# Selective scan, four experts and an FFN on one core: each token to its own expert, C by DMA, the product on GpSimd, the sum over states on TensorE

## The chip, the core and the metric

The kernel runs as one program on one core of a Trainium2 chip. The time is that of the device for one execution, in microseconds (us). A core has five engines that run their own instruction lists and meet only at semaphores: TensorE (PE; PEld is its weight load), VectorE (DVE), ScalarE (ACT), GpSimd (POOL) and SyncE (SP, which here only issues DMAs). Each list is executed in the order in which it is written: an instruction that waits holds back all behind it on that engine.

## The reference

Eight sequences x[b] of 1024 tokens, 128 channels. Layer one is a selective scan with 16 states per channel, followed by a mixture of four experts:

```
delta = softplus(x @ Wd + bd);  B = x @ WB + bB;  C = x @ WC + bC;  A = -exp(A_log)
h[s]  = clip(exp(min(delta*A[s], 2)) * h[s] + clip(delta*B[s], -2, 2) * x, -100, 100)   # over tokens
y     = sum_s h[s] * C[s] + x * D_param
route = softmax(y @ Wr + br);  top = argmax(route)
hid_e = silu(y @ up_w[e] + up_b[e]);  out_e = hid_e @ down_w[e] + down_b[e]      # 128 -> 512 -> 128
moe   = out_top * route[top]
x1    = norm(x + norm(y + moe) * ln_w + ln_b)
out   = norm(x1 + ffn(x1)),  ffn = (silu(x1 @ wg.T) * (x1 @ wu.T)) @ wdn.T        # int weights / 127, 384 hidden
```

The reference computes all four experts for each token and picks one. Only the picked one reaches the output.

## The kernel before

A sequence (batch) is one unit of work: tiles are 128 channels by 1024 tokens, or 128 tokens by 128 channels, eight of these to a batch. A batch goes through four stages, and an iteration runs four different ones side by side: `P` (projections, delta, B and C, and the bound that tells whether a clip could act) of batch i+1, `A` (the scan) of batch i, `B` (router, experts, first half of the norms) of batch i-1, `C` (norms and FFN) of batch i-2.

Stage A sets the frame. For each of the 16 states, PE spreads row s of B over all partitions (`psB`, two matmuls of 512 columns, line 382) and row s of C (`psC`, the same line); ACT makes `decay` (564); DVE multiplies `dx` into `psB` (662), runs the scan over tokens into `state` (849), and multiplies `state` by `psC` into `prod` (858); POOL adds `prod` to `yacc` (940), 15 times and a last time into `y`. `psB` and `psC` are single: the spread of state s+1 waits until the scan of s has read `psB`. On DVE the product of line 858 stands between the scan of s and the multiplication of s+1. `bc_parts` (822) and `dx` (823) are made at the batch's start.

Stage B computes all four experts for all tokens: for each of 2 halves of 512 tokens and 4 experts, `up` (437, four fp32 matmuls of 512 columns, each two instructions in the trace), `silu` (ACT 582, four of 128x512), `down` (444 for the bias, 451 for 16 fp32 matmuls of 128 columns), `weigh` (DVE 769, by 0 or the routing weight) and `mix` (POOL 893). The router's few columns ride in `y_turn` (430); lines 736 to 759 are its DVE part. The weights of all experts lie in SBUF from the start.

The order of each engine is a table per engine (`PE_STEPS`, `ACT_STEPS`, `DVE_STEPS`, `POOL_STEPS`) that hangs tasks on the 32 half steps of the scan. DMAs are few: per batch `xT` twice, `x` and the output.

The bound at the end of P (lines 716 to 732: `bound`, a scan as `majorant`, line 723, and a flag) chooses between the fast scan and a slow one token by token; in the profiled execution all scans are the fast ones.

## Time and profile before

| | |
|---|---|
| time, median of 3 runs | 1067.1 us (1066.87 to 1068.94) |
| time of the profiled execution | 1068.36 us |
| its span, first to last instruction | 1066.4 us |
| mean granted TensorE clock | 0.881 |
| busy share of the span, PE / DVE / ACT / POOL | 78% / 82% / 57% / 53% |
| DMA | 20.76 MB, 19 GB/s over the span |

An engine's share counts its own instructions, register and semaphore work left out. The span has a start (setup and stage P of batch 0), eight scans, and an end (what is left of batches 6 and 7), so shares over the whole span mix stretches with different limits; the table of stretches below is cut where the scans of the batches begin (the `dx` of line 823).

### The profile page before, as it was taken

To read this page: it belongs to the slowest core of one execution; us is meant where nothing else is said; L and a number is where in the kernel's file an instruction comes from. 1 tells how busy PE (TensorE), PEld (TensorE's weight loads), DVE (VectorE), ACT (ScalarE), POOL (GpSimd) and SP (SyncE) were. 2 spreads that over 40 slices of the span, in tenths; PEclk is the share of its full clock that TensorE was granted. 3 is DMA by queue.
4 is the path that set the end of the run, shared out by engine and by line. 5 is a ranking of instruction groups with operands and counts; after the bars stand their busy time and mean duration, and the time that the engine had idled before them with its cause. 6 is when DMAs were issued, how large, how long until landed. Compare 5 with 4: busy or idle time off the path is not lost.

```text
span 1066.4 us, 11980 instructions
## 1 busy us (share of the span) xinstructions
PE 835.7 (78%) x4059; PEld 521.1 (49%) x4120; DVE 878.6 (82%) x1173; ACT 609.3 (57%) x838; POOL 561.6 (53%) x412
## 2 busy tenths in 40 slices
PE   2354599768888789869897799869897789989973
PEld 1010256446555455546464455546554555657552
DVE  4999988699899998899899898999889999962332
ACT  5362177446866378456776278456775367525432
POOL 1255356555666465564576366564566466644232
PEclk8565699879998899979999899989998899989996
DMA  4100100010000100000000100001000100000000
GB/s 135 40 1 1 59 1 1 1 49 12 10 1 11 50 13 8 1 27 34 21 2 10 50 11 11 1 17 43 21 1 10 31 11 11 21 1 20 1 11 20
DMA packets 23046, 20.76 MB, mean 19 GB/s; under 512 B 2227, under 2 KB 19891, under 8 KB 22966
## 3 DMA queue, kind: packets, MB, share of 16 engines
q1 hardware_dynamic: 22966, 19.84, 5.9%
q8 instruction: 32, 0.52, 0.2%
q14 instruction: 48, 0.39, 0.1%
HBM read 15.64 MB, written 4.19 MB: 19 GB/s over the span
## 4 chain that ended last, share of the span: by engine, by line
DVE 37%; PE 34%; issue 13%; ACT 12%; POOL 2%; DVEq 1%; SPq 0%; DMA 0%; ACTq 0%; POOLq 0%
PE psU L437 15%; DVE state L849 11%; DVE psB L662 8%; PE psD L451 4%; ACT decay L564 3%; DVE prod L858 3%; PE psU L470 3%; PE psB L382 2%; DVE bst L791 2%; PE psU L471 2%; DVE weighed L769 2%; DVE inp L723 2%; PE psT L451 2%; PE psU L397 2%; PE psC L382 1%
## 5 line engine op out<-in xcount | busy, mean ns | idle before, releaser
L940 POOL TENSOR_TENSOR yacc<-prod,yacc 128x1024 f32<-128x1024 f32 x112 | 271.1, 2421 | 170.3 <-DVE prod L858 170.0
L849 DVE TENSOR_TENSOR_SCAN state<-decay,psB 128x1024 f32<-128x1024 f32 x128 | 292.7, 2287 | 13.2
L582 ACT ACTIVATE hid<-psU,upb_sb 128x512 f32<-128x512 f32 x256 | 175.7, 688 | 221.6 <-PE psU L437 221.4
L437 PE MATMUL psU<-y,up_sb 128*128 128x512 f32 x512 | 263.6, 652 | 1.8 <-ACT hid L582 1.8
L382 PE MATMUL psB<-bc_parts,sel 128*128 128x512 bf16 x233 | 83.3, 436 | 125.8 <-DVE state L849 100.6
L662 DVE TENSOR_TENSOR psB<-dx,psB 128x1024 f32<-128x1024 f32 x128 | 156.6, 1223 | 20.4 <-PE psB L382 19.3
L858 DVE TENSOR_TENSOR prod<-state,psC 128x1024 f32<-128x1024 f32 x128 | 155.9, 1218 | 20.8 <-PE psC L382 15.8
L451 PEld LDWEIGHTS psD<-down_sb,hid 128*128 128x128 f32 x1280 | 159.7, 203 | 7.1 <-issue 2.7
L437 PEld LDWEIGHTS psU<-y,up_sb 128*128 128x128 f32 x512 | 95.0, 205 | 139.4 <-ACT hid L582 93.3
L451 PE MATMUL psD<-down_sb,hid 128*128 128x128 f32 x1280 | 159.2, 286 | 0.2
L564 ACT ACTIVATE decay<-next_delta,a_sb 128x1024 f32<-128x1024 f32 x128 | 136.3, 1135 | 1.5 <-DVE state L849 1.4
L382 PEld LDWEIGHTS psB<-bc_parts,sel 128*128 128x128 bf16 x256 | 20.5, 100 | 165.3 <-DVE state L849 123.3
L893 POOL TENSOR_TENSOR moe<-moe,weighed 128x512 f32<-128x512 f32 x48 | 72.5, 1511 | 44.7 <-DVE weighed L769 42.4
L382 PE MATMUL psC<-bc_parts,sel 128*128 128x512 bf16 x222 | 78.0, 423 | 20.0 <-DVE prod L858 17.6
L451 PEld LDWEIGHTS psT<-down_sb,hid 128*128 128x128 f32 x768 | 89.5, 192 | 4.9 <-issue 2.7
L451 PE MATMUL psT<-down_sb,hid 128*128 128x128 f32 x768 | 89.6, 275 | 0.1
L900 POOL TENSOR_TENSOR minus_mean<-mv,minus_one 128x4 f32<-128x4 f32 x48 | 9.7, 202 | 105.8 <-DVE ve L799 105.8
L940 POOL TENSOR_TENSOR yacc<-prod,xD 128x1024 f32<-128x1024 f32 x8 | 18.8, 2354 | 74.8 <-DVE prod L858 62.7
L811 DVE SCALAR_TENSOR_TENSOR hh<-psU,hh 128x512 f32<-128x512 f32 x48 | 32.6, 690 | 28.7 <-PE psU L471 22.2
L382 PEld LDWEIGHTS psC<-bc_parts,sel 128*128 128x128 bf16 x256 | 23.4, 103 | 61.3 <-DVE prod L858 35.4
L588 ACT ACTIVATE x1h<-psT 128x512 fp32r<-128x512 f32 x16 | 9.6, 597 | 74.5 <-PE psT L460 74.4
L602 ACT ACTIVATE hh<-psU 128x512 f32<-128x512 f32 x48 | 28.5, 597 | 38.8 <-PE psU L471 38.6
(118 smaller groups left out, 1134.6 us busy)
## 6 DMA issues: line engine op xcount, KB each, us to landing
xT_sb<-in_xT SPq DMA_DIRECT2D x8, 512.0 KB, 3.3
x_again<-in_xT SPq DMA_DIRECT2D x8, 512.0 KB, 4.3
xt<-in_x SPq DMA_DIRECT2D x16, 256.0 KB, 3.4
out<-x SPq DMA_DIRECT2D x16, 256.0 KB, 2.3
up_sb<-in_up_w SPq DMA_DIRECT2D x1, 1024.0 KB, 7.7
hid<-in_wg SPq DMA_DIRECT2D x1, 192.0 KB, 2.5
hid<-in_wu SPq DMA_DIRECT2D x1, 192.0 KB, 3.3
hid<-in_wdn SPq DMA_DIRECT2D x1, 192.0 KB, 3.5
```

Source lines behind the costliest of these rows:

```text
L382: mm = pe.matmul(half(ps, c), sel[:, which * S + s, :], half(bc_parts, c), start=True, stop=True)
L437: pe.matmul(bank[banks[f]][:, :], up_sb[:, e, f * 128:(f + 1) * 128], half(y, c), start=True, stop=True).then_inc(filled[banks[f]], 1)
L451: mm = pe.matmul(bank[d][:, j * 128:(j + 1) * 128], hid[:, k % 2, f, j * 128:(j + 1) * 128], down_sb[:, e * NF + f, :], start=False, stop= ...
L470: pe.matmul(bank[u][:, :], w[:, m * 128:(m + 1) * 128], x1h[:, :], start=True, stop=False)
L564: nc.scalar.activation(decay[:, s % NDECAY, :], next_delta[:, :], ACT.Exp, scale=a_sb[:, s:s + 1]).then_inc(decay_ready, 1)
L582: nc.scalar.activation(hid[:, k % 2, f, :], bank[u][:, :], ACT.Silu, bias=upb_sb[:, (k % E) * NF + f:(k % E) * NF + f + 1]).then_inc(drain ...
L662: v.tensor_tensor(psB[:, :], dx[:, :], psB[:, :], ALU.mult).then_inc(inp_ready, 1)
L811: v.scalar_tensor_tensor(out=hh[:, m, :], in0=bank[up][:, :], scalar=INV127, in1=hh[:, m, :], op0=ALU.mult, op1=ALU.mult).then_inc(drained ...
L849: v.tensor_tensor_scan(state[:, :], decay[:, s % NDECAY, :], psB[:, :], 0.0, ALU.mult, ALU.add).then_inc(state_ready, 1)
L858: v.tensor_tensor(prod[:, s % NPROD, :], state[:, :], psC[:, :], ALU.mult).then_inc(prod_ready, 1)
L893: g.tensor_tensor(dst, ytok[:, c * NJ:(c + 1) * NJ, 0:D] if e == 0 else dst, weighed[:, k % 2, :, :], ALU.add).then_inc(mixed, 1)
L940: g.tensor_tensor((y if s == S - 1 else yacc)[:, :], prod[:, s % NPROD, :], (xD if s == 0 else yacc)[:, :], ALU.add).then_inc(added, 1)
```

## The change

- **Experts.** Each token goes to its own expert only. Router: `yT_turn`, `logits`, then `rank` (PE, with a triangular matrix of ones: each token's place within its expert) and `slots` (DVE, eight small instructions). Tokens are sorted into blocks of 128 that belong to one expert; 1024 tokens make at most 8 + 3 = 11 blocks, and 11 are always computed. POOL writes the rows to DRAM by 8 indirect DMAs of 128 rows (`scatter`), SP reads them back as blocks (`rows`, 3 DMAs), PE turns them (`sort_turn`), `up` / `silu` / `down` / `result` run per block of 128 tokens, SP stores the results (`store`, 3 DMAs), POOL fetches each token's row by 8 indirect DMAs (`gather`), DVE combines (`combine`: output times weight plus y, 8 instructions). Weights aren't resident: SP reads a block's expert number into a register and loads 128x1156 fp32 (592 KB, up, down and biases) into one of three buffers, 11 per batch.
- **C and the product.** Rows of C go to DRAM once per batch (ACT's DMA) and SP reads each back to all 128 partitions (`c_wide`, 512 KB, 16 per batch, 3 buffers). POOL multiplies `state` by `c_wide` into `prod` (3 state buffers, 3 product buffers).
- **The sum over states.** PE adds the products by transposing them into one accumulator in PSUM (`psY`, 8 transposes of 128x128 per state, one more set for x*D_param), which also turns them to tokens; ACT copies it (`y_copy`).
- **Smaller parts.** `bc_parts`, `x_again`, the `majorant` scan and `weigh` / `mix` go. The bound on h becomes (delta + 1/min|A|)*|x|*max|B| (`widen`, one more pass of `bound`); the flag goes by a DMA of 2 KB. The rest of x1 in the FFN is formed on PE (`x_rest`) and copied by ACT, and the FFN's residual is added on PE (16 more matmuls of 128 columns per batch). The output's DMAs go from ACT.
- **The order.** One table per engine, SP included, now lists tasks with the batch they belong to; there are no half steps any more, and a task of the next batch may stand anywhere.

The core of the diff (of the tables that set the order, only the scan's part on DVE is shown):

```diff
-NDECAY = 8
-NPROD = 4
+NDECAY, NSTATE, NPROD, NC, NW = 6, 3, 3, 3, 3
...
+    (-2, "ff_mul", 0, 0), (0, "scan", 11), (-2, "ff_mul", 0, 1), (-2, "ff_mul", 0, 2), (-2, "stats", 1, 1), (1, "dx"),
+    (1, "over"), (0, "scan", 14), (1, "flag"), (0, "scan", 15), (1, "scan", 0), (-2, "ff_mul", 1, 0),
+    (-2, "ff_mul", 1, 1), (-2, "ff_mul", 1, 2), (1, "scan", 1), (-2, "stats", 1, 2), (1, "scan", 2), (1, "scan", 3),
+    (1, "scan", 4), (1, "scan", 5), (0, "router_shift"), (1, "scan", 6), (0, "slots"), (-1, "combine", 0),
+    (-1, "stats", 0, 0), (1, "scan", 7), (0, "router_pick"), (-1, "combine", 1), (1, "scan", 8), (-1, "stats", 1, 0),
...
+            def load_c(c, s):
+                g = S * c.n + s
+                if s == 0:
+                    sp_.wait_ge(c_stored, 16 * (c.n + 1))
+                wait(sp_, prod_ready, g - NC + 1)
+                sp_.dma_start(c_wide[:, g % NC, 0:c.w], c_rows[c.n % 2, s:s + 1, 0:c.w].to_broadcast([D, c.w])
+                              ).then_inc(c_in[g % NC], 16)
...
+                if name == "weights":
+                    (k,) = args
+                    q = c.blocks0 + k
+                    if k == 0:
+                        sp_.wait_ge(blocks_ready, c.n + 1)
+                    wait(sp_, result_ready, q - NW + 1)
+                    e = sp_.value_load(block_expert[0:1, c.n % 2, k:k + 1], min_val=0, max_val=E - 1)
+                    sp_.dma_start(weights[:, q % NW, :], w_pack[bass.ds(e, 1), :, :].rearrange("o p w -> p (o w)")
+                                  ).then_inc(weights_in[q % NW], 16)
...
+            def add_turned(c, term, src, first, last, done):
+
+                for j in range(c.tiles):
+                    mm = pe.matmul(psY[:, j, :], src[:, j * ROWS:(j + 1) * ROWS], ident[:, :], is_transpose=True,
+                                   start=(first and j % NJ == 0), stop=last, skip_group_check=True)
+                mm.then_inc(done, 1)
+
+            def add_state(c, s):
+
+                g = S * c.n + s
+                pe.wait_ge(prod_ready, g + 1)
+                add_turned(c, s, prod[:, g % NPROD, :], False, s == S - 1, summed)
...
-                if name == "up":
-                    c, e = divmod(args[0], E)
-                    for f in range(NF):
-                        fill(it, banks[f], stage, task, f // 2)
-                        pe.matmul(bank[banks[f]][:, :], up_sb[:, e, f * 128:(f + 1) * 128], half(y, c),
-                                  start=True, stop=True).then_inc(filled[banks[f]], 1)
+                if name == "up":
+                    (k,) = args
+                    (u,) = banks
+                    q = c.blocks0 + k
+                    pe.wait_ge(weights_in[q % NW], 16 * (q // NW + 1))
+                    pe.wait_ge(turned, c.groups0 + k // 4 + 1)
+                    fill(u, c, task)
+                    for f in range(NF):
+                        mm = pe.matmul(bank[u][:, f * ROWS:(f + 1) * ROWS], weights[:, q % NW, f * 128:(f + 1) * 128],
+                                       yT_sorted[:, k * ROWS:(k + 1) * ROWS], start=True, stop=True)
+                    mm.then_inc(filled[u], 1)
...
+                    pe.matmul(bank[d][:, 0:D], ones_row[:, :], weights[0:1, q % NW, W_DOWNB:W_DOWNB + D],
+                              start=True, stop=False)
+                    for f in range(NF):
+                        mm = pe.matmul(bank[d][:, 0:D], hid[:, k % 2, f, :],
+                                       weights[:, q % NW, W_DOWN + f * D:W_DOWN + (f + 1) * D],
+                                       start=False, stop=(f == NF - 1))
+                    mm.then_inc(filled[d], 1)
...
+                if name == "silu":
+                    (k,) = args
+                    q = c.blocks0 + k
+                    u = f"U{k % 2}"
+                    act.wait_ge(filled[u], fills(u, c, ("up", k)))
+                    for f in range(NF):
+                        ins = nc.scalar.activation(hid[:, k % 2, f, :], bank[u][:, f * ROWS:(f + 1) * ROWS], ACT.Silu,
+                                                   bias=weights[:, q % NW, W_UPB + f:W_UPB + f + 1])
+                    ins.then_inc(drained[u], 1)
+                if name == "result":
+                    (k,) = args
+                    (d,) = banks_of(c, ("down", k))
+                    act.wait_ge(filled[d], fills(d, c, ("down", k)))
+                    wait(act, stored, 16 * c.groups0)
+                    nc.scalar.activation(result[:, k, :], bank[d][:, 0:D], ACT.Copy).then_inc(drained[d], 1)
+                    act.wait_ge(drained[d], fills(d, c, ("down", k)))
+                    act.sem_inc(result_ready, 1)
...
+                if name == "combine":
+                    (h,) = args
+                    dve.wait_ge(gathered, 16 * (c.tiles0 + c.tiles))
+                    dve.wait_ge(router_steps, 7 * (n + 1))
+                    wait(dve, affine_steps[h], 3 * c.with_half[h])
+                    for j in range(c.hj):
+                        jj = h * NJ + j
+                        ins = v.scalar_tensor_tensor(out=moe[:, jj, :], in0=chosen_out[:, jj, :],
+                                                     scalar=top_w[:, n % 2, jj:jj + 1], in1=ytok[:, n % 2, jj, :],
+                                                     op0=ALU.mult, op1=ALU.add)
+                    ins.then_inc(mixed[h], 1)
...
+                if name == "prod":
+                    (s,) = args
+                    g = S * n + s
+                    if g == 0:
+                        pool.wait_ge(setup_dve, SETUP)
+                    pool.wait_ge(state_ready, g + 1)
+                    pool.wait_ge(c_in[g % NC], 16 * (g // NC + 1))
+                    wait(pool, summed, g - NPROD + 1)
+                    g_.tensor_tensor(prod[:, g % NPROD, w], state[:, g % NSTATE, w], c_wide[:, g % NC, w], ALU.mult
+                                     ).then_inc(prod_ready, 1)
...
+                if name == "scatter":
+                    (j,) = args
+                    if j == 0:
+                        pool.wait_ge(zeroed, 32)
+                        pool.wait_ge(slots_ready, n + 1)
+                        pool.wait_ge(y_copied, n + 1)
+                        for m in range(3):
+                            wait(pool, sorted_in[m], 16 * c.with_group[m])
+                        wait(pool, scattered, 16 * c.tiles0)
+                    g_.indirect_dma_start(rows_in, bass.IndirectOffsetOnAxis(slot[:, n % 2, j:j + 1].bitcast(U32), 0),
+                                          ytok[:, n % 2, j, :], None).then_inc(scattered, 16)
+                if name == "gather":
+                    (j,) = args
+                    if j == 0:
+                        pool.wait_ge(stored, 16 * (c.groups0 + len(c.groups)))
+                        for h in range(2):
+                            wait(pool, mixed[h], c.with_half[h])
+                    g_.indirect_dma_start(chosen_out[:, j, :], None, rows_out,
+                                          bass.IndirectOffsetOnAxis(slot[:, n % 2, j:j + 1].bitcast(U32), 0)
+                                          ).then_inc(gathered, 16)
```

In the rows below a name is followed by what is written and what is read; x4 means four such in a row.

ScalarE, in a batch in the middle, where the experts' silu stands between the decays (before: `hid` is silu, `decay` is exp, `x1h` a copy, `hh` the FFN's silu, `moe` a norm):

```order
L588 ACTIVATE x1h<-psT 128x512
L582 ACT_TABLE_LOAD
L582 ACTIVATE hid<-psU,upb_sb 128x512 x8
L602 ACTIVATE hh<-psU 128x512 x3
L594 ACTIVATE moe<-moe,shift,rstd 128x128 x4
L564 ACT_TABLE_LOAD
L564 ACTIVATE decay<-next_delta,a_sb 128x1024 x4
L582 ACT_TABLE_LOAD
L582 ACTIVATE hid<-psU,upb_sb 128x512 x8
```

And now (`result` is the copy of a block's output):

```order
L710 ACT_TABLE_LOAD
L710 ACTIVATE decay<-delta,a_sb 128x1024
L739 ACTIVATE yT_sorted<-psD 128x512
L749 ACT_TABLE_LOAD
L749 ACTIVATE hid<-psU,weights 128x128 x8
L757 ACTIVATE result<-psT 128x128
L739 ACTIVATE yT_sorted<-psD 128x384
L710 ACT_TABLE_LOAD
L710 ACTIVATE decay<-delta,a_sb 128x1024
L757 ACTIVATE result<-psT 128x128
L749 ACT_TABLE_LOAD
L749 ACTIVATE hid<-psU,weights 128x128 x4
```

The decays, four or five in a row before, now come one at a time between the silus, and a table load stands at each turn: 9 in an iteration before, 16 now.

GpSimd, before, around the end of a scan (`moe<-moe,weighed` is `mix`):

```order
L881 TENSOR_TENSOR bnd<-bnd,zb 128x512 x2
L940 TENSOR_TENSOR yacc<-prod,yacc 128x1024
L893 TENSOR_TENSOR moe<-moe,weighed 128x512
L940 TENSOR_TENSOR yacc<-prod,yacc 128x1024
L893 TENSOR_TENSOR moe<-moe,weighed 128x512
L940 TENSOR_TENSOR y<-prod,yacc 128x1024
```

And now, where the gathers and the first scatters stand among the products:

```order
L1070 TENSOR_TENSOR prod<-state,c_wide 128x1024
L1099 DMA chosen_out<-rows_out,slot 128x128 x3
L1070 TENSOR_TENSOR prod<-state,c_wide 128x1024
L1099 DMA chosen_out<-rows_out,slot 128x128 x5
L1070 TENSOR_TENSOR prod<-state,c_wide 128x1024
L1091 DMA rows_in<-ytok,slot 1408x128
L1076 TENSOR_TENSOR bnd<-bcf,parts 128x1024
```

The 16 additions of a batch have become 16 products, the additions of the experts' outputs are gone, and 16 indirect DMAs are issued from this engine; the first gather waits for the last store of its batch, with the products behind it.

TensorE, before, in the same part of a batch (`psB`, `psC` the spreads, 437 `up`, 451 `down`):

```order
L382 MATMUL psC<-bc_parts,sel 128x512 x2
L437 MATMUL psU<-y,up_sb 128x512 x4
L444 MATMUL psT<-bias_down,sel 128x512
L451 MATMUL psT<-down_sb,hid 128x128 x16
L382 MATMUL psB<-bc_parts,sel 128x512 x2
L382 MATMUL psC<-bc_parts,sel 128x512 x2
```

And now (480 adds a product, 473 is the spread of B, 596 and 599 `down`, 586 `up`):

```order
L473 MATMUL psB<-parts,sel 128x512 x2
L480 MATMUL psY<-ident,prod 128x128 x8
L596 MATMUL psT<-weights,ones_row 128x128
L599 MATMUL psT<-weights,hid 128x128 x4
L586 MATMUL psU<-yT_sorted,weights 128x128 x4
L608 MATMUL psD<-ident,attn 128x128 x4
L586 MATMUL psU<-yT_sorted,weights 128x128 x4
L473 MATMUL psB<-parts,sel 128x512 x2
```

Each piece of expert work between two spreads has become smaller, the spread of C is gone, and the addition of a product has come in; a spread has one order place only, so an addition that waits for POOL ahead of it holds it back.

## Rows read from the trace of the kernel before

**Rows 1.** The page's part 4: the chain that ended last, by engine.
```profile
DVE 37%; PE 34%; issue 13%; ACT 12%; POOL 2%; DVEq 1%; SPq 0%; DMA 0%; ACTq 0%; POOLq 0%
```

**Rows 2.** Stretches: start:end and length, busy us of each engine (instructions), clock, DMA.
```profile
core 0: us, PE busy (x) PEld busy (x) DVE busy (x) ACT busy (x) POOL busy (x), PEclk, DMA share, GB/s
0.00:31.70 31.70, 7.74 (x27) 3.51 (x27) 16.39 (x36) 20.07 (x22) 4.82 (x7) 0.78 0.39 113
31.70:119.00 87.30, 36.98 (x89) 8.43 (x91) 83.25 (x64) 29.77 (x30) 40.94 (x19) 0.54 0.04 13
119.00:233.80 114.80, 92.43 (x432) 57.20 (x439) 98.32 (x101) 67.87 (x83) 63.90 (x37) 0.87 0.04 14
...
476.10:596.30 120.20, 99.48 (x507) 63.43 (x515) 108.63 (x146) 76.53 (x105) 70.73 (x51) 0.94 0.06 18
...
838.40:953.00 114.60, 102.54 (x510) 66.30 (x519) 101.94 (x135) 61.10 (x92) 63.20 (x48) 0.93 0.04 13
953.00:1066.40 113.40, 87.08 (x467) 59.12 (x469) 33.32 (x123) 47.66 (x87) 35.01 (x47) 0.91 0.04 12
```

**Rows 3.** Groups of lines, 476.1 to 596.3: busy us, mean ns | idle before, releaser.
```profile
L849 DVE TENSOR_TENSOR_SCAN state<-decay,psB 128x1024 f32<-128x1024 f32 x16 | 36.6, 2287 | 1.7
L940 POOL TENSOR_TENSOR yacc<-prod,yacc 128x1024 f32<-128x1024 f32 x14 | 34.0, 2431 | 16.8 <-DVE prod L858 16.8
L437 PE MATMUL psU<-y,up_sb 128*128 128x512 f32 x64 | 32.0, 634 | 0.6 <-ACT hid L582 0.6
L582 ACT ACTIVATE hid<-psU,upb_sb 128x512 f32<-128x512 f32 x32 | 21.9, 688 | 27.7 <-PE psU L437 27.7
L662 DVE TENSOR_TENSOR psB<-dx,psB 128x1024 f32<-128x1024 f32 x16 | 19.6, 1224 | 2.9 <-PE psB L382 2.7
L858 DVE TENSOR_TENSOR prod<-state,psC 128x1024 f32<-128x1024 f32 x16 | 19.5, 1218 | 2.8 <-PE psC L382 2.5
L451 PE MATMUL psD<-down_sb,hid 128*128 128x128 f32 x160 | 18.7, 275 | 0.0
...
L893 POOL TENSOR_TENSOR moe<-moe,weighed 128x512 f32<-128x512 f32 x6 | 9.6, 1592 | 3.7 <-DVE weighed L769 3.4
...
L382 PE MATMUL psC<-bc_parts,sel 128*128 128x512 bf16 x27 | 8.7, 389 | 1.8 <-DVE prod L858 1.4 <-issue 0.2
...
L769 DVE TENSOR_TENSOR weighed<-psD,top_w 128x512 f32<-128x512 f32 x5 | 3.4, 673 | 0.0
...
L916 POOL TENSOR_TENSOR moe<-moe,lnb_sb 128x512 f32<-128x512 f32 x2 | 2.6, 1278 | 0.2
...
L723 DVE TENSOR_TENSOR_SCAN inp<-sp,bnd 128x1024 f32<-128x1024 f32 x1 | 2.3, 2282 | 0.0
...
L905 POOL TENSOR_TENSOR shift<-minus_mean,rstd 128x4 f32<-128x4 f32 x6 | 1.2, 200 | 1.0 <-POOL rstd L902 1.0
```

**Rows 4.** Timeline of ScalarE: start, duration us, what.
```profile
546.46 1.64 ACT L594 ACTIVATE moe<-moe,shift,rstd 128x128 f32<-128x128 f32 x4
548.11 1.28 ACT L564 ACT_TABLE_LOAD   x1
549.41 4.27 ACT L564 ACTIVATE decay<-next_delta,a_sb 128x1024 f32<-128x1024 f32 x4
```

**Rows 5.** Timeline of TensorE: a spread of B at either clock, four transposes.
```profile
66.30 0.60 PE L382 MATMUL psB<-bc_parts,sel 128*128 128x512 bf16 x2 [1.56 <-DVE state L849]
...
87.24 1.04 PE L382 MATMUL psB<-bc_parts,sel 128*128 128x512 bf16 x2 [2.49 <-DVE state L849]
...
1024.48 0.60 PE L460 MATMUL psT<-ident_wr,x 128*128 128x128 f32 x4
```

**Rows 6.** Line 756 alone (VectorE, two SBUF inputs): duration ns, min/median/max.
```profile
L756 DVE TENSOR_TENSOR top_w<-rcode,rsmall x8: 141/2147/2152, 140.3 to 965.0; 128x32 f32<-128x32 f32 x8
```

**Rows 7.** DMA: the queue's total (MB, share of 16 engines), and issues with us to landing.
```profile
q1 hardware_dynamic: 22966, 19.84, 5.9%
...
xT_sb<-in_xT SPq DMA_DIRECT2D x8, 512.0 KB, 3.3
```

1273 lines of the change are left out of this document (713 added, 560 removed), and 32 rows, old and new, of tables (ACT_STEPS, DVE_STEPS, PE_STEPS, POOL_STEPS).

## The prediction, made before the changed kernel was run

> **What bounds the kernel now.** I read three views. The chain [rows 1] names DVE (37%) and PE (34%) and leaves POOL at 2%: POOL's long waits for products cost nothing. The table of stretches [rows 2] gives the limit by stage. A full batch takes 120.2 us, of which DVE works 108.6, PE 99.5, ACT 76.5, POOL 70.7, so DVE is the bound and is idle 11.6 us. Batch 0's scan takes 87.3 us, also DVE (83.3), at a low clock (0.54) with PE only 37.0 us busy. The second takes 114.8, the last 114.6, the start 31.7, the end 113.4; the five between average 120.9 (from 233.8 to 838.4). The groups of lines [rows 3] say what each engine does in a full batch. DMA is at 6%, no limit.
>
> **DVE.** Gone: 16 products, 19.5 us; 8 `weigh` at 0.67, 5.4; the majorant scan, 2.3 [rows 3]. Smaller ones gone (the reduction after that scan, the copy of parts, the subtraction and residual of the FFN, two router instructions) I put at 8 us, from DVE's 1218 ns for 1024 columns and 673 for 512 [rows 3] and line 756's 2.1 [rows 6]. New: two more half passes of `bound` (1.4 by the 673), 8 `slots` instructions and the flag's, small ones of 0.14 to 0.2 (2.0 in all, by line 756's shortest), 8 `combine` of 128 columns, between that 0.14 and the 0.67 (2.3). 108.6 - 35.2 + 5.7 = 79.
>
> One cost stands only indirectly in the trace. Line 756 has two SBUF operands and 32 columns; it took 0.14 us once and 2.15 at the median [rows 6], which is close to a whole POOL addition (2.4) [rows 3]. Twelve new DVE instructions have two SBUF operands (8 `combine`, 1 in the router, 3 in `slots`), and POOL will be busy three quarters of the time. From nothing to 12 x 2.0 = 24 us; most will meet POOL in the middle of something or not at all, and I take 6. DVE: 85.
>
> The Trainium skill says it as a rule ("SBUF — State Buffer", Who interferes with whom): a VectorE instruction with two SBUF inputs contends with a GpSimd one that reads SBUF, and one of the two is blocked for the other's whole length. The trace agrees (2.15 against 0.14 us). By the rule scan and multiplication, each with an operand in PSUM, stay free.
>
> **The gap between scans.** `psB` is single. Before, the product (1.2 us) covered the spread of the next row of B: 0.60 us at the high clock, 1.04 at the low [rows 5], and DVE waited only 2.9 us a batch for it [rows 3]. Now DVE goes from scan to multiplication with nothing between at four places of its table (15 to 0, 2 to 3, 3 to 4, 4 to 5): 0.7 each with the semaphore, 3 us. At the others another task covers. A spread held behind work of PE is in the idle time, which I keep at 12 of the 11.6. DVE's own sum is then 85 + 3 + 12 = 100.
>
> **PE.** Gone per batch: `up` 32.0; `down`, of which 160 instructions take 18.7, so all 256 take 29.9; the spreads of C 8.7; the biases 3 (8 of about 0.38, the length of a spread's half) [rows 3]; the old turn of y, 16 instructions at 0.12 or more, 2. That is 76 of 99.5. New: adding is 17 x 8 transposes. Four took 0.60 us [rows 5], so one more costs about 0.11 (`down` gives 18.7/160 = 0.117) and eight about 1.04: 17.7 us. A block's `up` is 4 fp32 matmuls, 8 instructions: 0.27 for the first and 7 x 0.117, 1.1; its `down` 10, 1.3; 11 blocks, 26.6. Turns, ranks, logits, the FFN's extra parts: some 70 instructions at 0.117, 8 us. 99.5 - 76 + 52 = 76 us at clock 0.94.
>
> **ACT.** Gone: 32 silu, 21.9 [rows 3]; the three copies of the old turn at about 0.5, 1.4. New: 44 silu of 128 columns. A 128-column norm in a group of four takes 1.64/4 = 0.41 [rows 4], a 512-column silu 0.688; 384 columns fewer at about 0.83 ns leave 0.37, less in a row; I take 0.31: 13.6. Eleven `result` 3.1, copies to turned tiles, y and x1 (9 of about 0.6) 5.3. Table loads: 16 for 9, 7 x 1.28 = 9.0. 76.5 - 23.3 + 31.0 = 84 us. ACT is the closest second.
>
> A load's cost is 1.28 here: it starts 0.01 us after the norm before it ends and the decay 0.02 after it [rows 4]. The Trainium skill ("ScalarE: Activation LUTs", What ACT_TABLE_LOAD costs) has 1283 ns and about 1380 ns of drain, 2.66 in all. By that, ACT would have 16 x 1.38 = 22 us more. The trace shows no such gap.
>
> **POOL.** Additions become products of the same size, 39 us for 39. `mix` goes: 8 calls, 9.6 and 2.5 us, 12. 70.7 - 12 = 58.6. New: 16 indirect DMAs to issue. No row has one; the nearest are POOL's smallest instruction, 0.20 us, and its largest, 2.43 [rows 3]. I take 1.28, that of a 128x512 instruction, for descriptors of 128 rows: 20 us, so 79 (62 to 98). The first gather waits for the last store of its batch; behind it wait the products from state 4 on, for them PE's additions, and, three states on, the scan. The Trainium skill ("DMA: Bandwidth & Descriptors", Specifications) gives about 1 us to the first byte on GpSimd's path; by that as an issue price POOL would be 75.
>
> **SP and DMA.** 27 big loads (16 of 512 KB, 11 of 592 KB), with rows, stores, x and out: 19 MB per batch. Before, 19.84 MB took 5.9% of 1066 us on all 16 engines [rows 7]: 315 GB/s, so 60 us per batch, 58% used. Loads of 512 KB land in 3.3 us alone [rows 7], and each C row has two states, over 10 us. Hidden, if the same 4 KB row read 128 times is no slower; if each load went alone, 16 x 3.3 + 11 x 4 = 97 us, still under the period.
>
> **The sum.** A full batch: DVE's 100, with three other engines at 76 to 84 that in-order lists couple to it; before, PE at 83% already stood in that idle time. I add 3: **103 us**, for 120.9. Batch 0's scan: 87.3 - 19.5 - 5 (copy, majorant) + 16 bare gaps of 1.1 at the low clock = 80. Second and last stretch in proportion (0.855): 98 each. The start stays 31.7: setup and the same projections. The end: 113.4 holds 62 us of dense `up` and `down`, now 11 blocks at about 2.4 us through PE, ACT, PE, ACT, 27: -35. It gains four DMA trips of about 3.3 (scatter, rows, store, gather), 13; 16 issues on POOL, 20, of which 2 overlap; router and slots in a chain, 3. About 112. Sum: 31.7 + 80 + 98 + 5 x 103 + 98 + 112 = 934.7; with the 2.0 us that lie outside the span (1068.36 - 1066.4), 936.7, and the profiled run was 1.3 above the median. **Forecast 935 us**, 12% faster.
>
> **Rivals.**
> 1. Waits overlap better. Port conflicts near nothing, POOL at 65: 92 us a batch. 31.7 + 75 + 88 + 460 + 88 + 100 + 2 = 845. For it: DVE has only 79 us of work. Against: four engines at 75 to 85 leave little slack. Chance 0.20.
> 2. POOL becomes the bound. At 2.4 us per indirect DMA it works 97 us; with 12 idle, 110 a batch: 31.7 + 80 + 103 + 550 + 103 + 120 + 2 = 990. For it: nothing here prices these DMAs, and the products wait behind them. Not faster than before only from (120 - 12 - 58.6)/16 = 3.1 us each. Chance 0.15.
> 3. The slower side: the clock stays down. In the scan of batch 0 PE was 42% busy and had 0.54, the lower level of 1.2 GHz most of the time; at 77 to 83% busy it had 0.87 to 0.94 [rows 2]. Work on PE falls by a quarter and consists of small pieces between waits. At the low level a spread takes 1.04 for 0.60 [rows 5], 1.7 times; PE's 76 become 129, with 12 idle 141 a batch: 31.7 + 85 + 125 + 705 + 135 + 125 + 2 = 1209. It decides from a mean clock of about 0.66, where PE's 76 become 108. Against: 76 of 103 is 74% busy, nearer to the stretches with 0.87. Chance 0.10, with 0.02 for POOL beyond 3.1 us: slower 0.12.
> 4. ACT becomes the bound, because a turn from exp to silu and back costs twice the load's row where it comes 16 times (ACT must finish one thing before the next, and no longer does four decays in between): 16 x 1.3 more, 84 + 21 + 11 = 116 a batch; 31.7 + 80 + 110 + 580 + 110 + 118 + 2 = 1032. Against: no such gap in the rows of the load [rows 4]. Chance 0.02. The Trainium skill's drain, above, is this rival.
> 5. It comes out even (a mix of 2 and 3): 0.02. That the change doesn't do what it says would show as scans by the slow path, hundreds of us each; its conditions are those of before. Under 0.01.
>
> The forecast has the remaining 0.49. Its own range is 96 to 110 us a batch, 880 to 990. For 8 in 10 I go from 848 (rival 1) to 1055, past rivals 2 and 4, leaving out most of rival 3. About 0.2% is what this measurement can tell from no change. Faster 0.86, same 0.02, slower 0.12.
>
> **What would show it.** Stretches between the `dx` of neighbouring batches of 96 to 110 us, DVE 82 to 90 busy in each, ACT 80 to 88, PE 70 to 85 at a clock of 0.8 or more, POOL 72 to 86. DVE instructions with two SBUF inputs far above 0.2 us would show the port's cost; DVE's waits before line 1040 for PE, the gap's; POOL's for C, a DMA limit; line 1099's issues, rival 2. I am wrong if the period follows PE at a clock under 0.7, if scans wait for products that stand behind gathers, or if C rows arrive late.

## The result, and the profile after

| | before | changed |
|---|---|---|
| time, median (4 runs each on the same chip) | 1068.0 us (1066.9 to 1069.5) | 1100.7 us (1099.3 to 1106.3) |
| ratio, 95% interval | | 1.031 (1.028 to 1.035), slower |
| span of the profiled execution | 1066.4 us | 1104.5 us |
| mean granted TensorE clock | 0.881 | 0.779 |

The forecast was 935 us, and the time lies outside its range (848 to 1055). The profiled execution of the changed kernel is the longest of its four (1106.3 us; the others 1099.3 to 1101.3). The tables of stretches say where the time is. Those of the changed kernel, cut at the first multiplication of each batch's scan (columns as in [rows 2]):

```profile
0.00:34.70 34.70, 9.18 (x27) 3.96 (x27) 12.35 (x36) 20.63 (x22) 4.82 (x6) 0.74 0.36 100
34.70:116.80 82.10, 41.40 (x182) 27.78 (x183) 64.19 (x49) 28.50 (x28) 44.26 (x18) 0.65 0.31 109
116.80:220.20 103.40, 66.09 (x373) 50.59 (x372) 74.94 (x68) 50.25 (x78) 51.43 (x27) 0.73 0.48 159
565.90:683.60 117.70, 87.12 (x541) 69.63 (x540) 88.92 (x132) 82.87 (x142) 75.50 (x59) 0.80 0.50 160
802.50:917.00 114.50, 80.85 (x512) 65.58 (x511) 76.42 (x116) 66.39 (x125) 67.90 (x56) 0.81 0.48 149
917.00:1104.50 187.50, 99.91 (x577) 78.63 (x575) 35.72 (x165) 62.07 (x161) 58.72 (x76) 0.74 0.24 73
```

and two of the kernel before, cut the same way (a full batch, and what follows the end of the last scan):

```profile
477.40:597.60 120.20, 99.51 (x508) 63.43 (x515) 108.60 (x144) 76.53 (x105) 70.73 (x51) 0.94 0.06 19
942.00:1066.40 124.40, 96.04 (x506) 65.06 (x509) 37.87 (x129) 51.34 (x94) 38.61 (x49) 0.90 0.04 11
```

Up to the end of the last scan the changed kernel is 25 us ahead (917.0 for 942.0). The drain behind it takes 187.5 us for 124.4, 63 more, and 63 - 25 = 38 is the difference of the spans. A full batch was to fall from 120 to 103 us and fell to 117.7: VectorE lost 19.7 us of work (108.6 to 88.9) and gained 17.2 of idle time (11.6 to 28.8). What the reader is to see is that in the full batch no engine is busy more than 76% of the time. The waits of that stretch (total us, times, longest) spread over all of them:

```profile
POOL prod L1070 <- DVE state L1043: 36.1, 8, 8.9
PEld psB L473 <- DVE state L1043: 16.3, 5, 6.6
DVE psB L1040 <- PE psB L473: 13.6, 7, 4.3
PE psB L473 <- DVE state L1043: 13.5, 5, 5.7
ACT moe L769 <- POOL shift L1113: 13.0, 2, 8.1
DVE holder L912 <- PE psT L532: 8.1, 1, 8.1
```

TensorE waits 13.5 us for a scan before it may spread the next row of B, and VectorE waits 13.6 for spreads, for 2.7 before [rows 3]: each in turn is late for the other. The groups of lines of that stretch that answer to [rows 3] (busy us, mean ns, idle before):

```profile
L1043 DVE TENSOR_TENSOR_SCAN state<-decay,psB 128x1024 f32<-128x1024 f32 x16 | 36.6, 2287 | 1.6
L1040 DVE TENSOR_TENSOR psB<-dx,psB 128x1024 f32<-128x1024 f32 x16 | 19.6, 1226 | 14.5 <-PE psB L473 13.6 <-issue 0.4 <-DVE clip_flag L922 0.2
L586 PE MATMUL psU<-yT_sorted,weights 128*128 128x128 f32 x88 | 13.2, 303 | 0.0
L599 PE MATMUL psT<-weights,hid 128*128 128x128 f32 x88 | 12.7, 288 | 0.0
L596 PE MATMUL psT<-weights,ones_row 1*128 1x128 f32 x22 | 5.3, 320 | 1.2 <-ACT hid L749 0.8 <-ACT result L757 0.4
L749 ACT ACTIVATE hid<-psU,weights 128x128 f32<-128x128 f32 x44 | 12.5, 368 | 3.7 <-PE psU L586 3.4
L1091 POOL DMA_INDIRECT rows_in<-ytok,slot x8 | 8.4, 1054 | 3.6 <-issue 3.6
L903 DVE TENSOR_TENSOR parts<-bnd,parts 32x1024 bf16<-32x1024 f32 x1 | 6.0, 5957 | 0.0
```

Most prices of the prediction hold in these rows: `up` and `down` with its bias (line 596) 31.2 us for 26.6, which at the measured clock (0.80 for 0.94) would be 31.3; silu 12.5 for 13.6; an indirect DMA about 1.25 us from one issue to the next (in its usual place 0.96 and 0.30 of idle time) for 1.28. One row was not priced at all: L903 (`bc_low`, two SBUF inputs) took 5.96 us for a work of 1.22. GpSimd held it, and for longer than one of its instructions. The timelines of VectorE and GpSimd there (start, duration):

```profile
638.81 5.96 DVE L903 TENSOR_TENSOR parts<-bnd,parts 32x1024 bf16<-32x1024 f32 x1
644.80 0.69 DVE L1023 SCALAR_TENSOR_TENSOR hh<-psU,hh 128x512 f32<-128x512 f32 x1
```

```profile
637.74 4.72 POOL L1070 TENSOR_TENSOR prod<-state,c_wide 128x1024 f32<-128x1024 f32 x2
642.43 1.25 POOL L1124 TENSOR_TENSOR moe<-moe,lnw_sb 128x512 f32<-128x512 f32 x1
643.76 2.13 POOL L1126 TENSOR_TENSOR moe<-moe,lnb_sb 128x512 f32<-128x512 f32 x1
```

Two products and L1124 stand back to back, and L903 gets through only at about 643.7, where L1126 has to wait for L1124's result. L1126 then takes 2.13 us, for 1.25 to 1.28 in the drain: it is now the held one.

The drain, in the chain of the changed kernel (start, duration; left out are pieces under 0.9 us and repeats): batch 6's last blocks, its gathers, its mixing and norm; batch 7's scatters with batch 6's affine steps between them; batch 7's blocks with the loads of their weights; its gathers; its norms.

```profile
935.56 1.10 PE psT L599 x8
...
940.72 0.95 POOL chosen_out L1099
...
948.21 5.24 DMA chosen_out<-rows_out,slot
...
961.10 1.05 POOL rows_in L1091
962.18 1.27 POOL moe L1124
...
976.28 2.23 DMA rows_in<-ytok,slot
978.53 2.80 DMA y_sorted<-rows_in
...
989.62 4.90 DMA weights<-in_w_pack
...
1000.25 5.83 DMA weights<-in_w_pack
...
1045.66 2.59 DMA chosen_out<-rows_out,slot
```

The same view of the kernel before has, in its drain, dense TensorE work back to back:

```profile
969.96 7.43 PE psU L437 x16
...
977.45 3.73 PE psD L451 x32
...
986.47 7.45 PE psU L437 x16
```

TensorE is busy about as long in both drains (99.9 and 96.0 us, at clocks of 0.74 and 0.90). Before, that was 77% of the drain; now it is 53%.

### The profile page after: what moved, and what is told of

Read it like the earlier page. It is cut to its first block, busy times and chain, and to the rows that moved or that the text cites. A ratio compares the mean times of both kernels' runs of the same rounds, so it can differ in the third digit from the quotient of the medians.

```text
span 1104.5 us, 13970 instructions
## 1 busy us (share of the span) xinstructions
PE 723.8 (66%) x4320; PEld 563.2 (51%) x4320; DVE 705.4 (64%) x1078; ACT 636.3 (58%) x1108; POOL 601.4 (54%) x468
## 4 chain that ended last, share of the span: by engine, by line
PE 39%; DVE 24%; issue 13%; ACT 7%; DMA 6%; POOL 6%; SPq 1%; DVEq 1%; ACTq 0%; POOLq 0%
DVE state L1043 11%; PE psY L480 7%; PE psU L586 7%; DVE psB L1040 6%; PE psT L599 6%; PE psB L473 5%; PE psD L640 4%; DMA weights<-in_w_pack 3%; PE psT L596 2%; PE psU L624 2%; DVE bst L1008 2%; PE psU L625 2%; POOL rows_in L1091 1%; DVE moe L991 1%; ACT decay L710 1%
## 5 line engine op out<-in xcount | busy, mean ns | idle before, releaser
L1070 POOL TENSOR_TENSOR prod<-state,c_wide 128x1024 f32<-128x1024 f32 x128 | 305.2, 2388 | 280.4 <-DVE state L1043 265.7
L1043 DVE TENSOR_TENSOR_SCAN state<-decay,psB 128x1024 f32<-128x1024 f32 x128 | 292.7, 2287 | 13.6 <-DVE psB L1040 0.5
L1040 DVE TENSOR_TENSOR psB<-dx,psB 128x1024 f32<-128x1024 f32 x128 | 157.0, 1227 | 134.3 <-PE psB L473 124.4
L473 PE MATMUL psB<-parts,sel 128*128 128x512 bf16 x256 | 100.1, 482 | 159.7 <-DVE state L1043 159.6
L480 PE MATMUL psY<-ident,prod 128*128 128x128 f32 x1024 | 169.8, 327 | 28.8 <-POOL prod L1070 28.8
L480 PEld LDWEIGHTS psY<-ident,prod 128*128 128x128 f32 x1024 | 153.8, 174 | 47.4 <-POOL prod L1070 30.7
L710 ACT ACTIVATE decay<-delta,a_sb 128x1024 f32<-128x1024 f32 x128 | 142.2, 1142 | 11.0 <-DVE state L1043 5.9
L749 ACT ACTIVATE hid<-psU,weights 128x128 f32<-128x128 f32 x352 | 99.8, 369 | 51.2 <-PE psU L586 49.8
L586 PE MATMUL psU<-yT_sorted,weights 128*128 128x128 f32 x704 | 105.5, 302 | 8.4 <-DMA weights<-in_w_pack 6.8
L586 PEld LDWEIGHTS psU<-yT_sorted,weights 128*128 128x128 f32 x704 | 98.7, 217 | 15.9 <-DMA weights<-in_w_pack 8.8
L599 PE MATMUL psT<-weights,hid 128*128 128x128 f32 x704 | 104.7, 293 | 0.0
L599 PEld LDWEIGHTS psT<-weights,hid 128*128 128x128 f32 x704 | 87.6, 196 | 10.9 <-issue 0.7
L1091 POOL DMA_INDIRECT rows_in<-ytok,slot x64 | 65.1, 1017 | 39.5 <-issue 39.5
```

What stands on the lines that cost most here:

```text
L473: mm = pe.matmul(tokens(psB, c, h), sel[:, s, :], parts[:, c.n % 2, h * HALF:h * HALF + c.hw], start=True, stop=True)
L480: mm = pe.matmul(psY[:, j, :], src[:, j * ROWS:(j + 1) * ROWS], ident[:, :], is_transpose=True, start=(first and j % NJ == 0), stop=last, ...
L586: mm = pe.matmul(bank[u][:, f * ROWS:(f + 1) * ROWS], weights[:, q % NW, f * 128:(f + 1) * 128], yT_sorted[:, k * ROWS:(k + 1) * ROWS], st ...
L599: mm = pe.matmul(bank[d][:, 0:D], hid[:, k % 2, f, :], weights[:, q % NW, W_DOWN + f * D:W_DOWN + (f + 1) * D], start=False, stop=(f == NF ...
L710: nc.scalar.activation(decay[:, g % NDECAY, w], delta[:, n % 2, w], ACT.Exp, scale=a_sb[:, s:s + 1]).then_inc(decay_ready, 1)
L749: ins = nc.scalar.activation(hid[:, k % 2, f, :], bank[u][:, f * ROWS:(f + 1) * ROWS], ACT.Silu, bias=weights[:, q % NW, W_UPB + f:W_UPB + ...
```

## Experiments

All are timed against the kernel before on the same chip; the changed kernel's ratio is 1.031. "Period" is the mean of the last five of the seven intervals between first multiplications, the first two being shorter in every kernel: 116.5 us in the changed kernel, 120.9 before. "Drain" is the time from the end of the last scan. Both are read from one profiled execution each, and two executions with the same steady part (e7 and e10) differ by 2.2 us in the period, so differences under about 2 us say little by themselves.

**e1: an order of its own for the end.** Behind the last sum of batch 7 each engine follows a written list.

```diff
 # GpSimd, behind batch 7's last product
-gather(6) 0..7, scatter(7) 0, rstd, scatter(7) 1, affine(6), rstd, rstd, scatter(7) 2..7, ...
+scatter(7) 0..7, rstd, gather(6) 0..7, rstd, affine(6), ...
 # TensorE
-up/down(6) .. 10, yT_turn(7), logits(7), rank(7), x_turn(6), ff_up(6), sort_turn(7), up/down(7), ...
+yT_turn(7), logits(7), rank(7) between blocks of 6, up/down(7) 0..10, ff_up(6), ff_down(6), ...
```

> Same work; only the order of what is left after the last state's sum of batch 7 is written out anew on every engine: batch 7's router and its eight scatters go ahead of batch 6's gathers, batch 7's experts run without a stop, batch 6's two feed-forward halves follow them, in the hole in which batch 7's gathers and norms run. The steady part (to the end of the last scan, 917.0 us of the changed kernel's span) is untouched. Theory A (the whole loss against the kernel before, 187.5 us of drain for 124.4, is the order of the end: a steady order's places kept where no scan is left): the drain falls from 187.5 to 145-160 us, total 1060-1075. Rival B (the end is long because its chain of gathers, norms and matmuls at a low clock is long whatever the order): drain 180 or more, total within 1% of 1100.7.

Measured: ratio 1.034 (1.031 to 1.038), drain 183.9. Expectation A failed and rival B's numbers came, but this order had a fault of its own. GpSimd did its scatters at 941 to 951, but ScalarE's list then had batch 6's first norm ahead of results that batch 7's blocks wait for, and that norm waited for batch 6's gathers, now 14 us later.

**e2: one transpose of eight.**

```diff
-for j in range(c.tiles):
+for j in range(c.tiles if term < 0 or term == S - 1 else 1):
     mm = pe.matmul(psY[:, j, :], src[...], ident[:, :], is_transpose=True, ...
```

> Of every state but the last, one of the eight transposes is issued (the other seven columns of the sum are left out), so TensorE has 105 short matmuls less in a batch, 12 us at 0.11 each and up to 26 at the 0.25 of the low clock, out of 87 us busy of 117.7. All waits, DMAs and other engines' work stay. Theory A (TensorE's list in order, with the sums in front of the next B spread, sets the pace of a batch): period from 117.7 to 103-109 us, total 1010-1040. Rival B (VectorE blocked by GpSimd, or ScalarE, sets the pace): period 115-118, total 1085-1101. Rival C (fewer columns bring the granted clock down further and give the time back): clock below 0.75 in a batch and total within 1% of 1100.7.

Measured: ratio 1.019 (1.016 to 1.022), period 115.5, drain 181.0. The full batch:

```profile
560.50:676.80 116.30, 74.33 (x430) 55.37 (x435) 90.27 (x133) 82.74 (x142) 75.56 (x59) 0.77 0.52 163
```

TensorE has 12.8 us less work in it, the batch takes 1.4 us less, and the whole kernel 12.4 (1088.3 for 1100.7), half of it in the drain. TensorE's own work does not set the pace; theory A, as I had put it, is wrong. The numbers are those of rival B.

**e3: no silu.**

```diff
-nc.scalar.activation(hid[...], bank[u][...], ACT.Silu, bias=...)
+nc.scalar.activation(hid[...], bank[u][...], ACT.Identity, bias=...)
-nc.scalar.activation(hh[...], bank[u][...], ACT.Silu, scale=INV127)
+nc.scalar.activation(hh[...], bank[u][...], ACT.Copy, scale=INV127)
```

> Silu of the experts and of the gates is left out (Identity and Copy in its place, same shapes), so that no activation table has to be changed for it: some 10 to 12 loads of 1.28 us less in a batch, ScalarE from 83 to 68-72 us of 117.7. Theory A (TensorE's list and the single B tile couple the engines, ScalarE is only passed through by the experts' chain): period 113-117, total 1070-1095. Rival B (the table loads stand in the chain that sets the pace: state decays late, experts' silu late): period 103-109, total 1000-1040. If there are as many loads as before: no change.

Measured: ratio 1.027 (1.024 to 1.030), period 115.4, drain 184.8. Table loads fell from 106 to 17, and ScalarE by 17.6 us in the full batch (65.3 of 116.3); the batch by 1.4, the whole kernel by 4.4 (1096.3). ScalarE does not set the pace either.

**e4: two indirect DMAs for sixteen.**

```diff
 if name == "scatter": ...
+    if j > 0:
+        return
     g_.indirect_dma_start(rows_in, ...)          # the same for the gathers
```

> Of the eight scatters and eight gathers of a batch one each is issued (tokens of the other seven tiles are not moved, the mixing reads tile 0's rows), so GpSimd has 14 indirect DMAs less in a batch, 14 x 1.26 = 17.6 us of 75.5 busy of 117.7, and blocks VectorE's two-input instructions less. Theory A (TensorE's list sets the pace): period 112-117 us and drain shorter by 15-25 us (gathers and scatters stand alone there), total 1040-1085. Rival B (GpSimd's products arrive late behind series of indirect DMAs, or its use of the port blocks VectorE: 5.6 us for one 1.2 us instruction): period 100-108, total 960-1010.

Measured: ratio 0.983 (0.978 to 0.987), period 111.9, drain 167.7. GpSimd has 12.6 us less in the full batch, which is 6.2 shorter. It is between the two expectations: nearer to A in the period, and the drain is 19.7 shorter, as A had it. L903 is no longer held (its line: ns, min/median/max):

```profile
L903 DVE TENSOR_TENSOR parts<-bnd,parts x8: 1222/1277/1517, 21.6 to 735.1; 32x1024 bf16<-32x1024 f32 x8
```

for, in the changed kernel,

```profile
L903 DVE TENSOR_TENSOR parts<-bnd,parts x8: 1221/5606/8545, 21.7 to 757.9; 32x1024 bf16<-32x1024 f32 x8
```

so up to 4.3 of the 6.2 us may be that, and the cut does not separate it from the queue of GpSimd. (The profiled execution is the longest of four, 1058.0 us for a median of 1049.9.)

**e5: the B tile is free one scan earlier.**

```diff
-wait(pe, state_ready, S * c.n + s)                 # before a spread
+wait(pe, inp_ready, S * c.n + s)
-v.tensor_tensor(psB[:, w], dx[:, n % 2, w], psB[:, w], ALU.mult)
+v.tensor_tensor(inp[:, w], dx[:, n % 2, w], psB[:, w], ALU.mult)
-v.tensor_tensor_scan(state[...], decay[...], psB[:, w], ...)
+v.tensor_tensor_scan(state[...], decay[...], inp[:, w], ...)
```

> VectorE's multiplication writes a tile in SBUF instead of the B tile in PSUM in place, and the next B spread waits for that multiplication and no more for the scan behind it: the single B tile is free one scan (2.3 us) earlier for each state. Orders and everything else as in the changed kernel. Theory A (the single B tile and the spreads queued behind TensorE's bunches set the pace; 20 us a batch in which TensorE waits for a scan before a spread, 14 in which VectorE waits for a spread): period from 117.7 to 100-108 us, total 980-1030. Rival B (the spread's place in TensorE's list behind other work that waits for something else, not the tile, is what holds): period 113-118, total 1065-1100. Rival C (the scan now reads two inputs from SBUF and is blocked by GpSimd as L903 was): scans above 2.3 us, total above 1105.

Measured: ratio 1.087 (1.083 to 1.092), period 128.1: rival C. The profiled execution took 1176.8 us, the other three 1155.3 to 1164.4, so the period is some 2 us on the long side. Two lines of that execution, of all 128 scans and 48 shifts:

```profile
L1045 DVE TENSOR_TENSOR_SCAN state<-decay,inp 128x1024 f32<-128x1024 f32 x128 | 342.0, 2672 | 13.6 <-DVE inp L1042 0.5
...
L1115 POOL TENSOR_TENSOR shift<-minus_mean,rstd 128x4 f32<-128x4 f32 x48 | 35.5, 739 | 8.2 <-POOL rstd L1112 7.7 <-PE psY L481 0.3 <-DMA c_wide<-c_rows 0.2
```

The scan takes 0.39 us more than with its input in PSUM (2287 ns above), and GpSimd pays more than VectorE: its work in the full batch goes from 75.5 to 92.3 us. So the second SBUF input costs both engines, and what the single tile costs stays open, since this edit changes both.

**e6: the same tasks in other places.** Only the five tables differ. The new places are chosen with this trace's durations as costs (1.25 us for an indirect DMA, 1.3 for a table load, VectorE held while GpSimd works, 4 to 5 for a transfer). Part of GpSimd's table:

```diff
-gather 0, gather 1, gather 2, prod 4, gather 3 .. gather 7, prod 5, scatter 0, bc_rest, rstd, prod 6,
-scatter 1, affine 0, prod 7, rstd, rstd, scatter 2 .. scatter 7, prod 8, prod 9, affine 1, prod 10, ...
+gather 0 .. gather 6, prod 4, gather 7, scatter 0, prod 5, scatter 1, prod 6, rstd, scatter 2,
+affine 0, scatter 3, rstd, scatter 4 .. scatter 7, rstd, prod 7, bc_rest, prod 8, affine 1, prod 9, ...
```

> The same instructions, all five order lists rewritten (each list keeps each batch's own sequence of states, blocks and halves; what changes is where one batch's work stands between the other's). The new places are chosen by the changed kernel's own durations: 1.25 us for an indirect DMA, 1.3 us for an activation table load, VectorE's two-input instructions held while GpSimd works, TensorE at a clock of 0.8, 4 to 5 us for a transfer. Theory A (the loss is in the lists' places, fixed for other durations than these, so that engines of 75-89 us busy wait for each other for 29 us of 117.7): same busy times, period 101-108 us, drain 170-190, total 985-1040. Rival B (the period is set by a resource the lists don't show, such as the clock, which falls as TensorE's work gets denser, or DMA latency under load): period 114 or more, total 1070-1110.

Measured: ratio 0.973 (0.970 to 0.976), that is 1038.0 us; period 108.8, drain 184.3. A full batch:

```profile
528.60:638.60 110.00, 81.97 (x541) 65.97 (x542) 84.14 (x133) 75.66 (x135) 76.58 (x58) 0.86 0.54 175
```

Moving tasks alone took 7.7 us off the period: theory A holds for the steady part, though the period is 0.8 us above its range. But busy times were not the same. Table loads fell from 106 to 70, VectorE was held less (84.1 for 88.9), and TensorE's clock rose (0.86 for 0.80), against what rival B supposed. Seen from VectorE, over the five intervals of the period, 4.2 of the 7.7 us are work (88.3 to 84.1) and 3.4 are idle time (28.1 to 24.7). So over half of the gain goes with instructions that are held less, and not with engines that wait less for each other; the places decide both, and this run does not separate them.

**e7: places once more, and a half waits for its own gathers.**

```diff
-gathered = sem("gathered")
+gathered = [sem(f"gathered{h}") for h in range(2)]
-dve.wait_ge(gathered, 16 * (c.tiles0 + c.tiles))
+dve.wait_ge(gathered[h], 8 * (c.tiles0 + c.tiles))
```

> The order lists of e6 gone over once more with what its trace added (GpSimd's elementwise work is itself held while VectorE has two inputs from SBUF: 1.71 us for 1.26 in L1125 of e6; about 0.1 us more for each wait that has to be woken), and the mixing of each half waits for its own four gathers, not for all eight. Theory A (places in the lists set the pace): busy times as in e6 (PE 80, VectorE 84, ScalarE 76, GpSimd 76), period from 108.9 to 100-105 us, drain 175-185, total 985-1025. Rival B (e6 has taken what order can give; the rest is waking times and the clock): period 107-110, total 1030-1045.

Measured: 1018.0 us (1017.1 to 1021.4), ratio 0.953 (0.951 to 0.954); period 107.6 in the profiled execution, its last two intervals 105.7 and 105.2; drain 174.7. The first of these two:

```profile
532.50:638.20 105.70, 79.65 (x547) 64.71 (x545) 85.74 (x133) 75.27 (x136) 76.52 (x59) 0.89 0.57 181
```

VectorE is idle 20.0 us, for 28.8; over the five intervals 21.9, for 28.1, and its work is 85.7. By the total this is theory A; by the period of its own profile it is rival B, by that of e10, 105.4 with the same steady part, nearly A. Tables and semaphore changed together, so the gain over e6 is not divided between them. This version is faster than both kernels: 4.7% below before, 7.5% below the changed kernel (1018.0/1100.7).

**e8: e7 with an end of its own.** From state 8 of batch 7 on, a written list again, without e1's mistake.

```diff
 # GpSimd, behind batch 7's last product, in e8
+rstd, scatter(7) 0..4, gather(6) 0, scatter(7) 5..7, gather(6) 1..7, rstd, affine(6), ...
```

> As e7, and what is left from state 8 of batch 7 on is put in an order of its own: batch 7's first scatters ahead of batch 6's gathers, its experts in one run, batch 6's feed-forward halves behind them, and no norm of batch 6 on ScalarE ahead of a result that batch 7's experts wait for, which is what stopped e1 (its second expert block waited until 6's gathers had landed). Theory A (in the end the lists' places cost as much as in the steady part): drain of 150-165 us, total 12 to 25 below e7. Rival B (the end is one chain through the router, scatters, sorted rows, eleven blocks, gathers, norms and two feed-forward halves of the last batch, which no order shortens): within 8 us of e7.

Measured: ratio 0.962 (0.960 to 0.964), 1027.6 us, 9.6 slower than e7. The drain is 168.9, 5.8 shorter, but the last scan ends 10.6 us later; the list has blocks of batch 6 ahead of spreads and sums of batch 7, which is the likely reason and was not tested. Neither expectation; the drain alone speaks for rival B.

**e9: L903 with one input.**

```diff
-v.tensor_tensor(parts[96:128, n % 2, w], rest[96:128, w], parts[96:128, n % 2, w], ALU.subtract)
+v.tensor_scalar(parts[96:128, n % 2, w], rest[96:128, w], 1.0, None, ALU.mult)
```

> The changed kernel with the third bf16 part of B and C made from one input (the subtraction of the second part is left out, the result is the rounded remainder itself), so that VectorE's L903 has one SBUF input and is not held by GpSimd: 1.2 us for 5.6. Theory A (a place in the lists sets the pace, and VectorE waits 9 to 13 us a batch around there anyway): period 115-118, total within 0.7% of 1100.7. Rival B (blocked VectorE instructions are on the path of every batch): 4.4 us less a batch, total 1060-1075. If L903 still takes over 3 us, it is not the second input that holds it.

Measured: ratio 1.028 (1.025 to 1.030), period 115.0, theory A's numbers. But it did not do what it was meant to:

```profile
L903 DVE TENSOR_SCALAR parts<-bnd x8: 690/4901/5426, 22.0 to 751.1; 32x1024 bf16<-32x1024 f32 x8
```

With one SBUF input the instruction is faster when free (0.69 for 1.22 us) and still held when GpSimd works. So the run tests neither theory, and how much of the period the hold costs is not settled by it.

**e10: TensorE kept busy in the end of e7.**

```diff
+def warm(count):
+    for _ in range(count):
+        pe.matmul(psB[:, 0:HALF], sel[:, 0, :], parts[:, 0, 0:HALF], start=True, stop=True)
 # before x_turn(n, 0) of batches 6 and 7:
+    warm(16)
+    for s, value in ((gathered[0], ...), (mixed[0], ...), (normed[0], ...), (affine_steps[0], ...), (rstd_ready[0], ...)):
+        pe.wait_ge(s, value)
+        warm(10)
```

> As e7, with extra work for TensorE in the end alone: in its two holes of 23 and 25 us (before batch 6's and batch 7's first x turn) it multiplies into the B tile, which nobody reads any more, 16 matmuls of 512 columns at once and 10 after each step of the norm's chain (gathers in, mixed, first norm, affine, second rstd), 66 in each hole, so that it is busy up to the turn that it waits for. Theory A (in the end TensorE's pieces stand on the chain at the low clock, 0.72 granted over the drain, because it idles ahead of them): the pieces behind the holes run at 0.11 us a block matmul for 0.21, drain from 174.7 to 160-169, total 1003-1013. Rival B (the clock does not follow, or the bursts come in late and hold the turns): drain 173 or more, total 1016-1030.

Measured: ratio 0.952 (0.949 to 0.955), 1016.3 us, the same as e7 within the intervals; drain 174.2. Batch 7's blocks, first in e7, then here:

```profile
895.00:950.00 55.00, 46.80 (x303) 38.49 (x304) 8.55 (x35) 30.08 (x84) 11.54 (x18) 0.91 0.38 118
```

```profile
889.00:942.00 53.00, 44.64 (x307) 37.31 (x309) 8.55 (x35) 28.12 (x83) 8.36 (x14) 1.00 0.39 119
```

The clock did follow, to 1.00 over the blocks, and gave 2 us there and 0.5 in the drain as a whole: rival B. Behind the second hole it fell to 0.74 all the same (0.73 in e7), so the last two feed-forward halves, 25 us of TensorE's work, were not tested at the high level.

**e11 and e12: e2's and e4's cuts in e7's order.** In e12 two scatters and two gathers a batch stay.

```diff
 # e11: e7 with e2's edit
 # e12
+    if j % NJ > 0:
+        return
```

> The order of e7 with e2's cut: of every state but the last one transpose of eight (seven columns of the sum left out). In the changed kernel's own order the same 13 us less of TensorE in a batch gave 1.0 us of period. Theory A (with the places better fitted, the lists still couple the engines more than any engine's own work bounds them): period from 105.4-107.6 to 103-106, total 1000-1018. Rival B (now TensorE, 76 busy of 103, is what the batch waits for): period 95-100, total 935-980.

> The order of e7 with two scatters and two gathers a batch for eight and eight (the other tiles' tokens are not moved; each half mixes its first tile's rows), so 12 indirect DMAs of 1.25 us less in a batch. In the changed kernel's order 14 less gave 4.6 us of period and 19.7 us of the drain. Theory A (GpSimd's series hold products in the steady part, and stand one by one in the last batch's chain): period down by 2-6 us, drain from 174.5 to 155-162, total 955-995. Rival B (with the new places they are hidden in the steady part): period down by less than 1.5 us, drain as under A, total 996-1006.

Measured: e11 ratio 0.941 (0.938 to 0.945), 1004.7 us, period 104.3, drain 172.2. e12 ratio 0.945 (0.941 to 0.948), 1009.1 us, period 106.1, drain 168.6. e7's period differs by 2 us between executions (107.6 in its own profile; 105.4 in e10's, which has the same steady part), so e11's cut is worth 1 to 3 us, as theory A had it, and e12's between -0.7 and 1.5. In e12 rival B holds for the steady part; of the drain 6.1 us went, not 12 to 20, and the total missed its range by 3. In e7's order, too, neither TensorE's nor GpSimd's own work is what a batch waits for. The pair e4 and e12 says one thing more: nearly the same cut took 50.8 us off the changed kernel, 19.8 of it in the drain, and 8.9 off e7, 6.1 of it in the drain. What GpSimd's indirect DMAs cost in the steady part, and the hold of L903 that goes with them (1.4 us at the median in e7, for 5.6), hung on where they stood.

## Why the prediction was wrong

By its own steps, with the working as it stands there:

- **Work of the engines: right.** In the full batch VectorE 88.9 us (85 forecast, range of the signs 82 to 90), ScalarE 82.9 (84), GpSimd 75.5 (79), TensorE 87.1 at clock 0.80 (76 at 0.94; at the measured clock that is 76 x 0.94/0.80 = 89).
- **Transfers: right.** GpSimd waits for states, not for C; c_wide lands in 4.9 us. Hidden, as forecast.
- **"12 of idle time", "3 us of bare gaps" and "I add 3": this step failed.** 18 us of VectorE's idle time were forecast, 28.8 measured. With the 3.9 us of its work above the forecast that is the whole difference of a full batch, 117.7 for 103. The waits of that batch show where: 13.6 us for spreads of B, where 3 were forecast, and 8.1 before `bound`, for TensorE's spread of B's maximum (line 912), for which no term stood. I had read the 11.6 us of [rows 2] as a cost that a change leaves alone. It belonged to a schedule in which VectorE worked 108.6 of 120.2 us, so that others waited for it. My reading is that with four engines at 64 to 76% of the period nothing absorbs a task that stands behind a wait. What the runs show is this: cuts of 12.8, 17.6 and 12.6 us on TensorE, ScalarE and GpSimd gave 1.4, 1.4 and 6.2 (e2, e3, e4); moving tasks with no work cut (e6) gave 7.7 on the period, and e7 came to 105.2 to 105.7 us in its last two batches, 2 to 3 above the forecast (107.6 over five). Part of what e4 and e6 gave is the hold of VectorE and not idle time, and how much is open.
- **Port conflicts, 6 us:** about right in sum, wrong in place. L903 alone cost 4.7 in that batch; the eight `combine` took 4.7 for 2.7 at their shortest (0.34). I had counted only new instructions and left out an old one, since it had never been held: before, the same subtraction (L709) took 1221 ns on average over its eight times.
- **The clock:** 0.94 was put into TensorE's 76 us, and 0.80 came. As far as tested it was no main cause of the loss: with 12.8 us less on TensorE the clock fell to 0.77 and the batch gave 1.4 us (e2), the 32 matmuls of a batch's spreads, the clock's direct place between two scans, took 458 ns each and 422 in e7 at 0.89, 1.2 us in all, and e10 raised it over the last blocks for 2 us there. No run raises it alone in the steady part or in the last 44 us.
- **The end, 112 us: this step failed too.** Cut as the prediction cuts it (from about 11 us behind the last scan) it took about 176, 64 more. The prediction subtracted 35 us for dense experts and priced the new parts one by one: blocks 27, trips 13, issues 20. It missed that batch 7's chain starts late and goes through the remains of batch 6: its last scatter is issued at 976, after 6's blocks, gathers, mixing and first norm. The eleven blocks took 53 us (981 to 1034) for 27, with two loads of weights on their chain (4.9 and 5.8 us, each issued when a result had freed a buffer) and one of batch 6's feed-forward halves among them. From there to the end, 70 us: gathers, six norms of half the tokens each, two feed-forward halves, each waiting for the one before.
- **What is left there:** of 187 us an order of its own took 4 (e1), better places with split gathers 13 (e7), an order of its own on top of these 6 more, which the scans before it paid back (e8), the higher clock over the blocks 0.5 (e10), 14 fewer indirect DMAs 20 (e4). So most of it seems to be one chain of dependent steps, longer than before, when dense TensorE work filled the drain. That is read from the chain and from these five bounds; a run that shortens the chain as a whole was not made, and the cause of the drain's 63 us stays open to that extent.

The sum, by the same parts: start +3, batch 0 +2, second +5, five full batches 582.3 for 515, +67, the last +28, the end +64: 170 before rounding, for a span of 1104.5 against the 934.7 summed. About 100 of it lies between start and last scan, 64 in the end. Of the 67 us of the five full batches VectorE's idle time above the 18 forecast is 50 (28.1 on average), its work above 85 is 17 (88.3).

Rivals: rival 2 priced indirect DMAs at 2.4 us, they took 1.25; but e4 shows that where they stand they do cost. Rival 3 (slower by the clock) had the sign and not the mechanism. Rival 4 did not occur: each load took 1.28 us, and behind 93 of the 106 the next instruction began 0.01 us later. Rival 1 gave too little room to waits, as the forecast did. What was missing among the rivals is the one that came: places in the lists that leave the engines waiting for each other and VectorE held, with a longer chain at the end. Its price could have been bounded from the trace: idle time between the old 11.6 us and the 41 us at which a batch would take the old 120 (120.2 - 79). That the old places were fitted to other durations than the chip's, as e6's expectation has it, no run shows.
